# A fused two-layer transformer kernel on one core: five instruction queues in a new order, and 51 products of constants instead of 19 between the layers

## The reference

```python
x = x + tanh(g_xattn[0]) * _L0_xattn_ref(_layernorm(x), ctx, ctx, ...)   # 16 heads of 8, causal mask
x = x + tanh(g_ffn[0])   * _L0_ffn_ref(_layernorm(x), ...)               # quantised 128 -> 512 -> 128
x = x + tanh(g_xattn[1]) * _L1_xattn_ref(_layernorm(x), ctx, ...)        # 8 keys for each head
x = x + tanh(g_ffn[1])   * _L1_ffn_ref(_layernorm(x), ...)               # 16 experts, best 2, and a shared one
```

## Time and profile before

| | |
|---|---|
| median of 3 runs | 175.63 us (175.36 to 176.75) |
| the profiled execution | 176.45 us, its span 174.6 us |
| TensorE busy | 161.4 us (92%) |
| VectorE busy | 122.1 us (70%) |
| ScalarE busy | 95.0 us (54%) |
| GpSimd busy | 78.9 us (45%) |
| mean granted TensorE clock | 0.971 |

### The profile page before, as it was taken

One profiled execution on the slowest core, in us unless ns is written; L12 is line 12 of the kernel. 1 busy time (PEld: TensorE's weight loads), 2 busy tenths in 40 slices (PEclk: granted clock), 3 DMA queues, 4 the chain that ended last, 5 costly groups with the idle time before them and its releaser, 6 DMA issues.

```text
span 174.6 us, 3885 instructions
## 1 busy us (share of the span) xinstructions
PE 161.4 (92%) x1430; PEld 98.9 (57%) x1441; DVE 122.1 (70%) x339; ACT 95.0 (54%) x180; POOL 78.9 (45%) x139
## 2 busy tenths in 40 slices
PE   7999999998989999999968659999999999999993
PEld 5645556754544455366646445547748675666573
DVE  0579777677987797878998684574787756836262
ACT  2259668579696878949579824332461333121210
POOL 8634565489889698888769630022000200000000
PEclk9999999999999999999999955799999999999999
DMA  5987000000000000000000000000000000100001
GB/s 157 398 273 332 4 2 4 6 2 4 0 4 0 0 4 0 4 2 4 2 0 0 4 0 0 0 0 2 4 0 0 0 0 0 60 4 0 0 0 60
DMA packets 1889, 5.82 MB, mean 33 GB/s; under 512 B 208, under 2 KB 592, under 8 KB 1744
## 3 DMA queue, kind: packets, MB, share of 16 engines
q1 hardware_dynamic: 1152, 4.01, 6.3%
q10 hardware_dynamic: 720, 1.57, 2.4%
HBM read 5.06 MB, written 0.52 MB: 32 GB/s over the span
## 4 chain that ended last, share of the span: by engine, by line
PE 73%; DVE 13%; issue 4%; POOL 4%; ACT 4%; POOLq 0%; ACTq 0%; DVEq 0%
PE banks L1546 11%; PE banks L1549 10%; PE banks L1572 10%; PE banks L1380 7%; PE banks L1368 4%; PE banks L1424 4%; PE banks L1389 4%; PE banks L1427 3%; DVE banks L919 2%; PE banks L1562 2%; PE banks L1408 2%; POOL vz L356 2%; DVE n L845 2%; PE banks L1398 2%; PE banks L1524 2%
## 5 line engine op out<-in xcount | busy, mean ns | idle before, releaser
L646 ACT ACTIVATE full<-banks 128x512 f32<-128x512 f32 x20 | 11.9, 596 | 30.0 <-PE banks L1546 29.9
L919 DVE TENSOR_REDUCE banks<-banks 128x8 f32<-128x1024 f32 x16 | 19.7, 1232 | 8.8 <-PE banks L1380 8.8
L289 POOL TENSOR_SCALAR_AFFINE_SELECT pT<-pT 128x512 f32<-128x512 f32 x32 | 20.3, 652 | 9.0 <-ACT pT L549 8.8
L1546 PE MATMUL banks<-nT,ews 128*128 128x512 f32 x40 | 22.1, 635 | 0.1
L1572 PEld LDWEIGHTS banks<-ews,rest 128*128 128x128 f32 x160 | 19.7, 192 | 3.3 <-issue 2.9
L1549 PE MATMUL banks<-nT,ews 128*128 128x512 f32 x40 | 21.3, 616 | 0.0
L549 ACT ACTIVATE pT<-banks 128x512 f32<-128x512 f32 x32 | 17.5, 595 | 5.7 <-PE banks L1408 5.5
L1572 PE MATMUL banks<-ews,rest 128*128 128x128 f32 x160 | 20.6, 277 | 0.0
L1086 DVE TENSOR_TENSOR rest<-xnT,banks 128x512 f32<-128x512 f32 x20 | 13.6, 683 | 9.6 <-PE banks L1562 4.6
L1078 DVE TENSOR_TENSOR xnT<-full,banks 128x512 f32<-128x512 f32 x20 | 13.6, 684 | 8.0 <-PE banks L1549 7.5
L1389 PE MATMUL banks<-qm,kT 32*128 32x512 f32 x64 | 16.9, 640 | 0.0
(11 more groups left out here) (174 smaller groups left out, 325.3 us busy)
## 6 DMA issues: line engine op xcount, KB each, us to landing
ews<-in_ew SPq DMA_DIRECT2D x1, 1928.5 KB, 7.8
fws<-in_fw SPq DMA_DIRECT2D x1, 768.0 KB, 8.1
cT<-in_ctxT ACTq DMA_DIRECT2D x2, 256.0 KB, 5.1
x_all<-in_x SPq DMA_DIRECT2D x2, 256.0 KB, 4.5
lws<-in_lw ACTq DMA_DIRECT2D x1, 449.0 KB, 8.3
sels<-in_sel ACTq DMA_DIRECT2D x1, 320.0 KB, 8.6
a<-in_aw ACTq DMA_DIRECT2D x1, 256.0 KB, 5.0
out_x<-x_all SPq DMA_DIRECT2D x1, 256.0 KB, 2.3
```

Of the source, the lines that this page charges most:

```text
L289: nc.gpsimd.affine_select(out=probs, in_=probs, compare_op=ALU.is_ge, fill=0.0, base=0, pattern=[[0, HG], [1, S]], channel_multiplier=-1). ...
L919: V.tensor_reduce(bank[2 * p][:, 0:2 * HG], banks[p][:, :].rearrange("p (h k) -> p h k", h=2 * HG), AX.X, ALU.max).then_inc(sm["a_mx"], 1)
L1546: mm(bank[u][:, :], expert(c)[0], nT4[:, s, :], start=True, stop=True).then_inc(sm["e_gp"], 1)
```

## The change

All five lists but SyncE's are put in a new order; no operation is added or removed but the products of constants between the layers, which go from 19 (counts 3, 2, 4, 5, 3, 2) to 51 (counts 7, 6, 5, 5, 9, 14, 5). The diff is long; its core is here, from the passage between the layers:

```diff
             hidden_dequant(5)
             bias_into_x(0)
+            nc.gpsimd.memset(wT[:, :], 0.0).then_inc(sm['wT_zero'], 1)
+            hidden_dequant(6)
             x_dequant(7)
-            hidden_dequant(6)
             rstd_of(2, 0)
             gated_up(7)
-            nc.gpsimd.memset(wT[:, :], 0.0).then_inc(sm['wT_zero'], 1)
             hidden_dequant(7)
...
             causal(7, 0)
-            rstd_of(1, 0)
             causal(7, 1)
             causal(7, 2)
+            rstd_of(1, 0)
             causal(7, 3)
             gated_up(5)
...
+            up_copy(7)
             gate_tanh(7)
-            up_copy(7)
+            hT_copy(6)
             tanh_plus_one(7)
...
             residual3(0)
+            ffn_stats(4)
+            ffn_stats(5)
             layer1_normalize(2, n4, 0, "n4r")
-            ffn_stats(4)
+            ffn_residual(6)
             hidden(7)
             hidden_steps(7)
-            ffn_residual(6)
...
-            keep_busy(2, 4)
             gate_up(7)
-            keep_busy(2, 5)
+            keep_busy(2, 9)
             h_transposes(6)
-            keep_busy(2, 3)
-            x4_transposes(0)
+            values_times_outputs(1)
             down(6)
-            keep_busy(2, 2)
+            keep_busy(2, 14)
+            x4_transposes(0)
+            keep_busy(2, 5)
             logits(0)
```

More of the change, by code:

```diff
@@ L778, in _ @@
             tanh_plus_one(6)
-            vo_copy(0)
             hT_copy(5)
+            kq_copy(1)
             pT3_copy(0)
             x_scaled(7)
-            nc.scalar.activation(table[:, 0:1], tg[:, 0:1], ACT.Silu)
+            xqT_copy(7)
             hidden_scale(6)
-            xqT_copy(7)
+            up_copy(7)
             gate_tanh(7)
-            up_copy(7)
+            hT_copy(6)
             tanh_plus_one(7)
-            kq_copy(1)
             vo_copy(1)
-            hT_copy(6)
             xT4_copy(0)
@@ L795, in _ @@
             shared_tanh(0)
+            chosen_tanh(0)
             expert_silu(0)
-            chosen_tanh(0)
             hT_copy(7)
+            wT_copy(0)
+            nc.scalar.activation(table[:, 0:1], tg[:, 0:1], ACT.Silu)
             expert_silu(1)
-            wT_copy(0)
             expert_silu(2)
@@ L1094, in _ @@
             q_masked(0, 0)
+            top(0, 0)
             q_masked(0, 1)
-            top(0, 0)
             split_max(0, 0)
@@ L1602, in _ @@
             subtract_max(0, 1)
-            heads(0, 0)
-            score_masks(1, 1)
-            max_rows(1, 0)
-            scores(1, 1)
-            transposed_scores(1, 0)
-            subtract_max(1, 0)
+            q_proj(1)
+            v_proj(1)
+            max_rows(1, 0)
+            score_masks(1, 1)
+            transposed_scores(1, 0)
+            scores(1, 1)
+            subtract_max(1, 0)
+            heads(0, 0)
             heads(0, 1)
-            q_proj(1)
             score_masks(2, 0)
@@ L1615, in _ @@
             subtract_max(1, 1)
-            v_proj(1)
+            layer1_proj(0)
             y_proj(0)
@@ L1619, in _ @@
             score_masks(2, 1)
+            max_rows(2, 0)
+            transposed_scores(2, 0)
             scores(2, 1)
-            transposed_scores(2, 0)
-            max_rows(2, 0)
-            layer1_proj(0)
-            layer1_proj(1)
             subtract_max(2, 0)
@@ L1627, in _ @@
             score_masks(3, 0)
-            max_rows(2, 1)
             scores(3, 0)
             transposed_scores(2, 1)
+            max_rows(2, 1)
+            layer1_proj(1)
+            y_proj(1)
             subtract_max(2, 1)
             heads(2, 0)
-            y_proj(1)
+            score_masks(3, 1)
+            max_rows(3, 0)
+            transposed_scores(3, 0)
+            scores(3, 1)
             xq_transpose(0)
-            score_masks(3, 1)
-            scores(3, 1)
-            transposed_scores(3, 0)
-            max_rows(3, 0)
             subtract_max(3, 0)
```

395 lines of the change are left out of this document (198 added, 197 removed).

## The result

The changed kernel takes **170.69 us** (median of 4 runs, 170.55 to 170.95); the kernel before, on the same chip, 175.63 us (4 runs, 175.36 to 176.75). The ratio is 0.9714 with a 95% interval of 0.9674 to 0.9753: faster by 2.9%. The profiled execution took 170.81 us and its span is 169.0 us, where 176.45 and 174.6 us stood.

A forecast was written before the change was run, and what follows sets the result against it. TensorE's own work bounds layer 0 and the experts; VectorE and its waits bound the passage, followed by a slow-clock stretch. -4.19 - 0.95 = -5.14 us takes the median 175.63 to 170.5 us; range 168.2 to 174.0.

The forecast's parts named there:

- the forecast one: Whole kernel: the clock holds and the time falls within 168.9 to 172.1 us; chance 0.60.
- The clock: From x4_transposes(0) to hidden_proj(1): products and moved work fill TensorE's idle stretch, so granted clock stays 1.00; -4.19 us.
- The second set: layer1_normalize(2, n4, 0), between the layers: the MEMSET moved ahead of rstd_of(2, 0) no longer prolongs the first normalisation; -0.95 us.
- The first set: Half 0's first four normalisations: rstd_of(1, 0) two causal later, one still caught by one long instruction; 0, between -0.96 and +0.85.
- The case that I feared: Half 0's first normalisations: one caught by both causal(7, 3) and gated_up(5), taking 2150 ns; 0.85 us more.
- Products as work: Between the layers: 32 more products of constants, 3.5 us, hidden in TensorE's waits; 0, at worst +1.54 us.
- The table load: ScalarE: load moved from the passage to between chosen_tanh(0) and expert_silu(0), covered there; 0, cover 0.67 us.
- Layer 0's order: Layer 0: reordered queues can change only TensorE's idle time; 0, at best -1.96, loss bounded at +2 us.
- the clock did not fall: Rival, passage: the clock falls all the same and only 0.95 us remain, 174.7 us; chance 0.12.
- nothing was given back: Rival, passage: normalisation caught twice and constants or table load uncovered, 172.1 to 173.9 us; chance 0.13.
- no new wait appeared: Rival, layer 0: causal(2, 1) behind x_dequant(0) holds heads(2, 0) and breaks the clock, 177.0 us at least; chance 0.06.
- More is gained: Rival: layer 0's idle time goes (-1.96) or normalisations meet nothing (-0.96), 167.0 to 168.9 us; chance 0.09.

The follow-up runs named there:

- products alone: Kernel before with only three counts of constant products raised (9 for 5, 18 for 3, 5 for 2; 41 in all): 172.9 us, ratio 0.9847.
- work in the gap: Kernel before, its 19 products unchanged, with values_times_outputs(1) and down(6) moved between h_transposes(6) and x4_transposes(0): 172.56 us, ratio 0.9822.

## Why the prediction was right, step by step

Forecast 170.5 us, measured 170.69; forecast gain 5.14 us, measured 4.94. The case was the forecast one: the clock held, and its gain came on top of an earlier start. That the sum came out within 0.2 us is luck, for two of its terms were off by about 1 us each, in opposite directions.

- **The clock, -4.19.** The mechanism holds: the clock falls where TensorE has no work ahead of the transposes, and it stayed at 1.00 with the gap filled. Between the profiled executions the slow stretch cost 3.8 us. The terms behind the logits came out in their sum, 2.64 us against 1.88 + 0.26 + 0.44 = 2.58: `hidden_proj(0)` gave 1.79, `h_transposes(7)` 0.41 and the first product of `hidden_proj(1)` 0.44. `x4_transposes(0)` and `logits(0)` did not come down to 0.44 and 0.86 but to 0.67 and 1.04 us; I had read their durations in the middle of dense work, and here each begins after a wait. By the medians the clock is worth less: 4.94 less the two parts below is 3.2 us, and the two kernels that change little but the clock gained 2.6 (products alone) and 3.0 us (work in the gap). So the term was too large by 1.0 to 1.6 us. Most of this has a source on record: I read the term off an execution with a mean clock of 0.971, which took some 0.9 us more than those with 0.98, and subtracted it from a median of which most runs have 0.98.
- **What holds the clock.** I named the products and the moved work together. Each is enough alone in a kernel with the long gap (172.9 and 172.56 us). In the new order, which already has the moved work, the clock fell with 19 products in one of four runs, and without any in the middle of the passage even in the best of six. With all 51 it held in every run of the changed kernel, but not in one of six once the MEMSET left an idle stretch of 1.31 us behind them. The work moved into the gap and 19 products kept the clock in one order and not always in the other, so a margin in this is not something that I could read off one profile.
- **The second set, -0.95.** Measured 0.76 for the MEMSET's place. The mechanism was as forecast: one normalisation caught by `gated_up(7)` alone, 1323 ns. That more could not be used "because the 14 products stand in front" was half of the reason: with 6 products and nothing caught only 0.34 us more came, and the rest was lost to the chain through `hidden(7)`. I also said that the MEMSET goes into time in which GpSimd waited. It delays `x_dequant(7)` there, which does no harm and helps to make `gated_up(7)` late.
- **The first set, 0 within -0.96 and +0.85.** This is the step that failed. I took "one is still caught by one long instruction" and it came out at the favourable end: **-0.97 us**, by moving that line back. The trace of before could have said more: VectorE came to the set 0.64 us ahead of `gated_up(5)`, and an undisturbed set takes 1.1 us, so half a microsecond more between the two gets it out of the way. The case that I feared, one caught by two instructions, did not arise even with three `causal` in succession.
- **Products as work, 0**, held: they end at 100.50 us, 0.06 before the normalisation, and 32 fewer gave 0.1 us in the three runs in which the clock held.
- **The table load, 0 in both places**, held twice. The trace after agrees with the earlier trace rows and not with the drain that the Trainium skill (ScalarE: Activation LUTs, What ACT_TABLE_LOAD costs) adds: the next activation starts at 105.92 us, 0.01 after the load's end.
- **Layer 0's order, 0 (up to 2 either way)**: 1.07 us faster, of which 0.97 hang on the line above. TensorE's own idle time there did not change (1.96 and 2.03 us).

0.76 + 0.97 = 1.73 us by the medians accounts for the start of the transposes, 1.71 us earlier in the profiles; since these differ by up to 0.3 us from their start on, the agreement to the hundredth is chance. The rivals: the clock did not fall, nothing was given back, and no new wait appeared. "More is gained" was there in part, hidden by the smaller worth of the clock.

## What to carry to other kernels

Where a slow clock sits behind an idle stretch of TensorE, fill that stretch, with the kernel's own work first, and time it in several runs: with a thin filling one kernel gave 170.6 and 172.65 us, and one profile shows only one of the two. Before a cost is read off a profile, see which kind of execution it is: the mean clock of each run told here that the profiled one took 0.9 us more than most, and that a median hid half and more of a gain of 0.7 to 1.1 us. Where two engines meet in a lock, look at which GpSimd instructions follow the release of a VectorE operation and when VectorE comes to it; and before delaying one, follow what else hangs on it.

## What the runs showed of the hardware that was not expected

- A VectorE normalisation of 128x128 f32 takes 0.34 us, 0.575 when a GpSimd `causal` of 0.64 us meets it, 1.32 beside a product of 1.27 us, and 2.15 to 2.24 beside that product and a MEMSET of 0.95 us directly behind it. Three `causal` in direct succession held one normalisation each (two at 0.67 us), and did not add up.
- The same program gets or loses the lower clock level from run to run: 170.58 and 172.65 us with 19 products, 171.4 and 173.06 us with 51 and an idle stretch, 170.22 and 173.9 us without any, and once 259.24 us at a mean clock of 0.562. In the new order with 19 products TensorE was dense and at 0.50 from 102.8 to 106.2 us; in the kernels with the long gap this lasted over 9 us.
- Four transposes in a row take 0.44 us in dense work and 0.67 us behind a wait, both at full clock, and the eight products of the logits 0.86 and 1.04 us.
